# Splitting the edge lists and bringing the first table emptying forward in a one-core graph-attention layer

## What is computed

```
x_norm = _layernorm(x, ln_g, ln_b)
q, k, v = ((x_norm @ W + b).reshape(N, H, HD) for each of Wq, Wk, Wv)
scores = jnp.einsum('ehd,ehd->eh', q[origin], k[destination]) * SCALE
ws = scores * edge_weights
seg_max = jax.ops.segment_max(ws, origin, num_segments=N)
e = jnp.exp(ws - seg_max[origin])
denom = jax.ops.segment_sum(e, origin, num_segments=N)
att = e / (denom[origin] + 1e-16)
values = jax.ops.segment_sum(att[:, :, None] * v[destination], origin, num_segments=N)
values = (values.reshape(N, D) @ W1 + b1) @ W2 + b2
return x + values
```

## Time and profile before

| | |
|---|---|
| median of 3 runs | 853.5 us (851.43 to 857.59) |
| the profiled execution | 854.37 us |
| its span in the trace | 851.2 us |
| granted TensorE clock, mean | 0.98 |
| PE busy | 782.4 us (92%) |
| DVE busy | 583.2 us (69%) |
| POOL busy | 457.5 us (54%) |
| ACT busy | 339.6 us (40%) |

### The profile page before, as it was taken

How to read it: one execution, slowest core, us unless ns; L and a number is a source line. 1 busy time by engine, 2 the same in 40 slices (tenths; PEclk the granted TensorE clock), 3 DMA queues, 4 the chain that set the end, 5 groups by cost and what they waited for, 6 DMA issues and landing times.

```text
span 851.2 us, 13484 instructions
## 1 busy us (share of the span) xinstructions
PE 782.4 (92%) x4751; PEld 458.3 (54%) x4791; DVE 583.2 (69%) x1331; ACT 339.6 (40%) x794; POOL 457.5 (54%) x391
## 2 busy tenths in 40 slices
PE   2999897899999999979999999999999999999993
PEld 2554445444446444435555555555556667666661
DVE  3487594954233503358888888998988978878886
ACT  0311301022312122035556555556555555545662
POOL 1028878778778877777777787777610001001000
PEclk9989999998999999979999999999999999999998
DMA  7697968897546569315353535435354143242203
GB/s 225 175 375 269 320 203 277 250 357 227 161 136 200 158 185 335 95 15 193 103 202 104 185 120 160 146 103 193 108 164 165 66 152 104 95 148 89 86 1 120
DMA packets 69632, 143.98 MB, mean 169 GB/s; under 512 B 20537, under 2 KB 54251, under 8 KB 65599
## 3 DMA queue, kind: packets, MB, share of 16 engines
q1 hardware_dynamic: 47084, 119.42, 39.9%
q0 software_dynamic: 13344, 6.28, 6.6%
q10 hardware_dynamic: 9136, 17.39, 6.2%
HBM read 77.99 MB, written 64.77 MB: 168 GB/s over the span
## 4 chain that ended last, share of the span: by engine, by line
PE 70%; DVE 21%; DMA 4%; issue 3%; ACTq 1%; ACT 1%; DVEq 0%
PE bank L890 17%; PE bank L884 12%; DVE AR L1540 11%; PE bank L1118 8%; PE bank L1085 8%; PE bank L1100 8%; PE bank L1090 4%; PE bank L1147 4%; DVE AR L1549 3%; DMA AR<-w_tab 2%; PE bank L998 2%; PE bank L873 1%; DMA AR<-in_L_gnn_b_dram 1%; PE bank L987 1%; PE bank L949 1%
## 5 line engine op out<-in xcount | busy, mean ns | idle before, releaser
L514 POOL DMA_INDIRECT w_tab<-pay,idx x330 | 403.9, 1224 | 153.3 <-issue 153.0
L765 ACT ACTIVATE AR<-AR,nmx 128x512 f32<-128x512 f32 (+1 forms) x240 | 159.0, 664 | 48.0 <-DVE nmx L1544 46.5
L1540 DVE CUSTOM_DVE_ANT_0 AR<-bank,AR,MX 128x512 f32<-128x512 f32 (+1 forms) x160 | 151.8, 986 | 20.0 <-PE bank L1090 19.1
L772 ACT ACTIVATE AR<-bank 128x512 f32<-128x512 f32 (+1 forms) x120 | 67.3, 561 | 173.9 <-PE bank L1100 173.9
L1085 PE MATMUL bank<-KT,QT 64*128 64x512 f32 (+1 forms) x480 | 118.3, 570 | 8.6 <-issue 5.3
L1100 PE MATMUL bank<-ident,AR 128*128 128x128 f32 (+2 forms) x880 | 122.7, 280 | 1.1 <-ACT AR L765 1.1
L1118 PE MATMUL bank<-AR,V 128*64 128x128 f32 (+1 forms) x1600 | 114.0, 280 | 6.1 <-DVE AR L1549 6.0
L884 PE MATMUL bank<-AR 128*128 128x512 f32 (+1 forms) x288 | 109.0, 538 | 7.3 <-ACT QT L642 3.2
L1118 PEld LDWEIGHTS bank<-AR,V 128*64 128x64 f32 (+1 forms) x1600 | 85.6, 136 | 52.3 <-issue 50.9
L890 PE MATMUL bank<-AR 128*128 128x512 f32 x240 | 108.3, 607 | 2.5 <-ACT AR L696 2.5
L1100 PEld LDWEIGHTS bank<-ident,AR 128*128 128x128 f32 (+2 forms) x880 | 94.0, 139 | 22.3 <-issue 15.9
(11 more groups left out here) (250 smaller groups left out, 755.2 us busy)
## 6 DMA issues: line engine op xcount, KB each, us to landing
w_tab<-ztile SPq DMA_DIRECT2D x20, 2280.0 KB, 15.0
AR<-w_tab SPq DMA_DIRECT2D x20, 2048.0 KB
AR<-w_tab SPq DMA_DIRECT2D x10, 1344.0 KB
w_tab<-ztile SPq DMA_DIRECT2D x3, 1800.0 KB, 13.2
w_tab<-pay,idx POOLq DMA_INDIRECT x330, 4.4
w_tab<-ztile SPq DMA_DIRECT2D x2, 1700.0 KB, 16.5
kv_rows<-AR ACTq DMA_DIRECT2D x9, 256.0 KB, 6.5
kv_rows<-V ACTq DMA_DIRECT2D x9, 256.0 KB
```

Of the source, the lines that this page charges most:

```text
L514: pool.indirect_dma_start(out=w_tab, out_offset=bass.IndirectOffsetOnAxis(ap=idx[:, k, j:j + 1], axis=0), in_=pay[:, k % RING, j, :], in_o ...
L765: act.activation(ws[u % 2][hh][:, 0:n], ws[u % 2][hh][:, 0:n], ACT.Exp, bias=nmx[:, u % 4, hh:hh + 1], accum_out=DG[g][:, c, 2 * p + hh:2 ...
L772: act.activation(PT[u % 2][0][:, 0:nb * P], bank[2][:, 0:nb * P], ACT.Copy).then_inc(s_ea, 1)
L1540: v.tensor_tensor_reduce(out=ws[u % 2][hh][:, 0:n], in0=bank[SB[(2 * u + hh) % 3]][:, 0:n], in1=Wt[w % 2][:, 0:n, h], scale=1.0, scalar=MX ...
```

## The change

Four things move. (1) The lists of edges are loaded in two parts: chunks 0 to 3 first, ahead of everything else on SP, then the weights and the emptying of chunk 0, then Wk, then chunks 4 to 21. (2) DVE converts the lists in two parts too: `edges(0, 4)` and `detect(0)` stand ahead of `take_x(0)`, `detect(1)` ahead of `moments(1)`, and the rest comes after `normed(1)`. SP waits for three chunks' indices, not one, before it loads `wchk`, since only then has the second part been read. (3) POOL gathers the losers' weights before chunk 20, not after chunk 21. (4) ACT loads the six bias columns ahead of Wq.

```diff
+FIRST = 4
...
             def load_edges():
                 for a, to in ((src, sW), (dst, dW)):
-                    sp.dma_start(to[:, 1:NCH, :], view(a, CE - HALO, ((CJ, QL), (CE, NCH - 1), (1, WIN)))).then_inc(s_edges, 16)
+                    sp.dma_start(to[:, 1:FIRST, :], view(a, CE - HALO, ((CJ, QL), (CE, FIRST - 1), (1, WIN)))).then_inc(s_edges, 16)
...
+            def load_other_edges():
+                for a, to in ((src, sW), (dst, dW)):
+                    sp.dma_start(to[:, FIRST:NCH, :], view(a, FIRST * CE - HALO, ((CJ, QL), (CE, NCH - FIRST), (1, WIN)))).then_inc(s_edgesb, 16)
...
+            load_edges()
+            load_weights_of_edges(0)
+            empty(0)
             sp.dma_start(sWk, wv(Wk)).then_inc(s_w4[1], 16)
-            load_edges()
-            for k in range(3):
+            load_other_edges()
+            for k in range(1, 3):
                 load_weights_of_edges(k)
                 empty(k)
-            sp.wait_ge(s_idx, 1)
+            sp.wait_ge(s_idx, 3)
             sp.dma_start(wchk, w_edge.rearrange("(p t) h -> p t h", p=QL)).then_inc(s_chk, 16)
...
             for k in range(NCH):
+                if k == NCH - 2:
+                    pool.wait_ge(s_lists, 1)
+                    for j in range(SLOTS):
+                        pool.indirect_dma_start(out=wx[:, j, :], out_offset=None, in_=w_edge,
...
+            pool.wait_ge(s_wx, 16 * SLOTS)
             pool.wait_ge(s_lists, 2)
-            for j in range(SLOTS):
-                pool.indirect_dma_start(out=wx[:, j, :], out_offset=None, in_=w_edge,
...
-            pool.wait_ge(s_wx, 16 * SLOTS)
...
-            act.dma_start(sWq, wv(Wq)).then_inc(s_w4[0], 16)
             for i, a in enumerate((ln_g, ln_b, bq, bk, mbq, b1)):
                 act.dma_start(crow[KC * i:KC * i + KC, :], a.rearrange("(k p) -> k p", p=P)).then_inc(s_col, 16)
+            act.dma_start(sWq, wv(Wq)).then_inc(s_w4[0], 16)
             load_x(1)
...
-            def edges():
-                dve.wait_ge(s_edges, 16 * 14)
+            def edges(a, b):
+                if a == 0:
+                    dve.wait_ge(s_edges, 16 * 14)
+                else:
+                    dve.wait_ge(s_edgesb, 32)
...
             normed(0)
+            edges(0, FIRST)
+            detect(0)
             dve.wait_ge(s_cols, 1)
             take_x(0)
             fold(0)
+            detect(1)
             moments(1)
             normed(1)
-            edges()
-            detect(0)
-            detect(1)
+            edges(FIRST, NCH)
             fold(1)
             order_checks()
```

More of the change, by code:

```diff
@@ L277, in gps_layer @@
         s_pad = sem("pads_ready")
-        s_edges = sem("edges_loaded")
+        s_edges = sem("first_edges_loaded")
+        s_edgesb = sem("other_edges_loaded")
         s_x = [sem(f"x_loaded{j}") for j in range(3)]
@@ L507, in _ @@
             for k in range(NCH):
+                if k == NCH - 2:
+                    pool.wait_ge(s_lists, 1)
+                    for j in range(SLOTS):
+                        pool.indirect_dma_start(out=wx[:, j, :], out_offset=None, in_=w_edge,
+                                                in_offset=bass.IndirectOffsetOnAxis(ap=e_idx[:, j:j + 1], axis=0),
+                                                bounds_check=E - 1, oob_is_err=False).then_inc(s_wx, 16)
                 if k >= 2:
@@ L516, in _ @@
                                             bounds_check=CELLS - 1, oob_is_err=False).then_inc(s_sc[k % 2], 16)
+            pool.wait_ge(s_wx, 16 * SLOTS)
             pool.wait_ge(s_lists, 2)
-            for j in range(SLOTS):
-                pool.indirect_dma_start(out=wx[:, j, :], out_offset=None, in_=w_edge,
-                                        in_offset=bass.IndirectOffsetOnAxis(ap=e_idx[:, j:j + 1], axis=0),
-                                        bounds_check=E - 1, oob_is_err=False).then_inc(s_wx, 16)
-            pool.wait_ge(s_wx, 16 * SLOTS)
             for j in range(SLOTS):
@@ L1185, in _ @@
             v.memset(wx[:, :, :], 0.0)
-            def edges():
-                dve.wait_ge(s_edges, 16 * 14)
[L1189 to L1193, removed]
+            def edges(a, b):
[3 more added lines that the diff above has]
+                    dve.wait_ge(s_edgesb, 32)
+                v.tensor_copy(oc[:, a:b, :], sW[:, a:b, HALO:WIN])
+                ch.link(v.tensor_copy(dc[:, a:b, :], dW[:, a:b, HALO:WIN]))
+                v.scalar_tensor_tensor(out=key[:, a:b, :], in0=sW[:, a:b, :], scalar=float(N), in1=dW[:, a:b, :], op0=ALU.mult, op1=ALU.add)
+                v.tensor_copy(dwin[:, a:b, :], dW[:, a:b, :])
+                ch.link(v.scalar_tensor_tensor(out=cell[:, a:b, :], in0=oc[:, a:b, :], scalar=float(COLS), in1=dc[:, a:b, :], op0=ALU.mult, op1=ALU.add))
             def detect(k):
```

## The result

The changed kernel takes 859.4 us (median of 9 runs, 856.1 to 864.3), the kernel before 853.5: a ratio of 1.0076, with a 95% interval from 1.0056 to 1.0096. It is slower by 0.8%, where 853.2 was forecast. The profiled execution took 862.2 us, its span is 860.2, 9.0 more than before. (On the chip 853.5 us is the median both of the three runs shown first and of nine.) The two traces thus differ by more than the medians do, 7.8 us in time and 9.0 in span against 5.9: what follows says where the loss lies in one execution of each, not its typical size.

A forecast was written before the change was run, and what follows sets the result against it. PE was taken as the bound, busy 782.4 of 851.2 us, with the scatters awaited by nobody. From 854.37 us, 0.4 for the front and 0.8 for the row stores came off, giving 853.2; the range was 846 to 860.

The forecast's parts named there:

- Part 5: Stores of k and v rows: gain 0.8 us (0 to 3.15); emptyings newly meeting weight loads near 165 us could cost 2.
- Reading of the bounds: Whole kernel: PE bounds it, busy 782.4 of 851.2 us; nobody waits for POOL's scatters, so starting them sooner gains nothing directly.
- Part 1: POOL's scatters: first near 25 us instead of 57.5, second chunk at 58, then 22 us ahead; value 0.
- Part 2: First weights: Wq shares with chunk 0's emptying, fold(0) starts about 15.0 us, 1.5 us earlier (-1.9 to 3).
- Part 3: DVE ahead of PE: early lists and detect(0) cost 0; detect(1) costs ACT 2.7 us against 1.58 spare; PE nets 0.4.
- Part 4: Second part of the lists: lands about 49 us, in time up to 59.8, so 0 us; later, each microsecond costs one.
- The list of what would show the prediction wrong: DVE idle over 15 us at late lists with PE waiting, fold(0) after 16.6 us, or changed attention pitch per tile.
- C: Rival: second part of the lists lands late, at 69 or 70 us, costing 10 us: 864.6 us; chance 0.08.
- A: Rival: nothing or small loss, the emptying slows Wq and detect(1) holds ACT back: 854.4 to 857.4 us; chance 0.20.
- B: Rival: all side effects help, at the front, stores, late tile and first k projections: 8.7 us, 845.7; chance 0.20.
- D: Rival: POOL's scatters are the bound and their 22 us come off: 832 us; chance 0.02.

The follow-up runs named there:

- b_early_again: Kernel before, but emptyings of chunks 11 and 12 may go after 4 scattered chunks instead of 5: 864.1 against 853.8 us, ratio 1.0113.
- a_hold_gather: Changed kernel with emptyings from chunk 11 on held until Mv has landed and the gather back behind the last chunk: 849.15 us, ratio 0.9947 to before.
- a_hold_again: Changed kernel with emptyings from chunk 11 on held until Mv has landed, second run: 847.5 against 853.8 us for the kernel before, ratio 0.9911.
- the first series: Four variants of the changed or earlier kernel (emptyings held, emptyings early, POOL delayed, detect(1) moved) on one chip, where the kernel before took 906.5 us.
- b_cols_first: Kernel before with only the six bias columns issued ahead of Wq on ACT's queue: ratio 0.9969 to the kernel before.

## Why the prediction was wrong, point by point

The forecast was 853.2 us, 0.3 under the median of before; the kernel got 5.9 us slower. The step that failed is in Part 5.

- **Reading of the bounds: right.** POOL isn't waited for. The last loser scatter came 17 us earlier (594.2; 611.4 before), and the attention kept its time within 0.7 us.
- **Part 1: right, with the lead too large.** First scatter at 27.05 (25 forecast), then the pause until 63.48 (58), and nothing gained. The second chunk started at 80.8 before, so POOL was 17 us ahead and not 22. The two rows of POOL:

```profile
27.05 1.39 POOL L529 DMA_INDIRECT w_tab<-pay,idx  x1 [22.64 <-issue]
...
63.48 1.19 POOL L529 DMA_INDIRECT w_tab<-pay,idx  x1 [13.73 <-DMA w_tab<-ztile]
```

- **Part 2: right sign, too small.** `fold(0)` began at 13.02, 3.5 us earlier instead of 1.5, just past the bound of 3:

```profile
13.02 6.98 PE L884 MATMUL bank<-cols,AR 128*128 128x1 f32 x32 [1.79 <-DMA AR<-in_L_gnn_Wq_dram]
```

  Wq was issued at 5.38 and landed 7.6 us later, at 13.0, beside chunk 0's emptying. The forecast let it start at 6.5, gave 6.9 for equal shares and 1.4 for the landing, 14.8 in all. Which of these was too long isn't told apart. The 3.5 us is near the upper end: in the other eleven traces with the changed front `fold(0)` begins between 12.9 and 14.6.
- **Part 3: the mechanism right, its net right by luck.** The first detection cost nothing, DVE still idled 4.35 us before `take_x(0)`. `detect(1)` held ACT; PE's rows:

```profile
43.04 1.15 PE L863 MATMUL bank<-ident,AR 128*128 128x128 f32 x8 [1.97 <-ACT AR L644]
44.02 6.56 PE L884 MATMUL bank<-cols,AR 128*128 128x1 f32 x32
50.44 16.01 PE L895 MATMUL bank<-AR 128*128 128x512 f32 x32
```

  `fold(1)` then took 6.56 against 4.67 us, with the granted clock at 0.54 from 44 to 48 us, where it was 1.00 before; the forecast had no such term. Of 3.5 us 0.3 were left at the first k projections (50.44; 50.74 before). The forecast had 0.4, from 1.5 less 1.1: two errors of about 2 us that cancel.
- **Part 4: right.** DVE stood still for the lists, and they came inside the bounds, at 55.7, ahead of 59.8:

```profile
55.71 0.30 DVE L1203 CAST oc<-V 125x270 f32<-125x270 int32 x1 [19.96 <-DMA V<-in_dst_dram]
```

  Twenty idle microseconds on DVE, and PE nowhere waits for them. The list of what would show the prediction wrong asked for PE's wait beside DVE's idle time, and that is the part that counts.
- **Part 5: this is the step that failed.** It gave the row stores 0.8 and "a new meeting of emptyings with the weight loads near 165 us" at most 2, outside the sum and without a reason for the 2. The 0.8 wasn't gained: the stores' stall stayed, 3.14 us and 7.17 behind it, as in the earlier trace rows:

```profile
145.21 7.17 PE L895 MATMUL bank<-AR 128*128 128x256 f32 x32 [3.14 <-ACT QT L653]
```

  The meeting cost 10.3 us in the trace (7.9 of wait and 2.4 of slow work), and PE's lead of 0.7 took a little off. Emptyings in that place cost 10.3 us in the kernel before, between medians (b_early_again), and the hold gave back 9.0 on one chip (a_hold_gather). It could have been worked out: Part 1 had POOL 22 us ahead; the issues of emptyings in the kernel before are 154.7, and a pair at 178.2 and 180.2; shifted by 22 the pair stands at 156 to 158, in front of loads that go at 165 (it went at 159 to 160). Two equal queues double Mk and Mv, and Mv's 10.5 us had only 3.0 of slack: 7.5 us of wait. I used the equal share for Wq in Part 2 and not here. That 7.5 is an estimate made afterwards, and it holds no term for the low clock behind a wait.
- **The rivals.** C's 10 us is near the meeting's cost, but for the wrong reason: late lists, which weren't late. A's 854.4 to 857.4 had the sign, for Wq, which was early. B and D fell. The range of 846 to 860 holds the median at its upper end, and 0.76% lies within the 1% that had 82%; but no case on the list gave that number for the reason that made it.

With the pair held, the rest of the change gains 0.4 to 0.9% (0.9962, 0.9961, 0.9947 and 0.9911). The columns bring 1.0 to 2.6 us of it; what the rest comes from isn't told apart. The profiled executions of a_hold_again and a_hold_gather are 2.8 and 3.9 us shorter in span than before's.

## What to carry to other kernels

An engine with slack still sets the time at which its consumers' DMAs are issued. When a change shifts it, take the trace's list of large issues, shift every row by that amount, and look which loads that PE waits for they land beside; price each by doubling the load's time and subtracting its slack. Leave some room in both: here POOL's lead was 16 to 17 us and the pair moved by 19 to 20, and the wait was followed by 2.4 us of slow work. A wait in the issuing queue for the load's own semaphore can keep them apart; here, for Mv, it cost nothing that the runs show, since the emptied ranges had time.

## What the runs showed of the hardware that was not expected

- Mk's load of 1 MB took 7.5 to 8.8 us with no emptying issued in the 9 us before it, 13.6 with one of 2.28 MB 3.5 us before it, and 14.4 to 16.1 with two or three. PE's start was at Mv's landing within 0.15 us in each of the seven runs with a wait outside the first series (after 186.4 and 186.45, b_early_again 189.06 and 189.14, b_cols_first 174.03 and 174.12, for instance).
- A wait costs more than its length. From the start of the loser bases to the first mask it is 181.6 to 183.4 us in the seven traces without a wait outside the first series, and 184.5 to 186.4 in the seven with one: 2.8 us more on average. In the changed kernel 2.4 of it are the matmuls that ran while the granted clock was at 0.50 behind the wait. In single groups a stretch at low granted clock shows as `fold(1)` of 3.6, 4.7, 5.3 or 6.6 us for the same 32 matmuls.
- On the first series' chip PE did up to a quarter less work in 363 to 509 us, while POOL scattered; the profile names a releaser "remote" there. No run here tells what that is.
